# A two-layer graph transformer on one core: in layer 2, P normalised before its transposes, and PV with V stationary in 64x32 tiles

## The reference

```python
q = (x @ Wq.T).reshape(b, n, 12, 32); k = (x @ Wk.T)...; v = (x @ Wv.T + bv)...
scores = einsum('bqhd,bkhd->bhqk', q, k) * scale + (adj + adj)[:, None]
row_nonzero = any(scores != 0, axis=-1, keepdims=True)
p = nan_to_num(softmax(where(row_nonzero, scores, -inf), axis=-1))
out = einsum('bhqk,bkhd->bqhd', p, v).reshape(b, n, 384) @ Wo.T + bo
x = layernorm(x + out)
```

## Time and profile before

| | |
|---|---|
| median of three runs | 1967.26 us (1966.64 to 1967.50) |
| profiled execution | 1970.78 us, of which 1968.9 us are the span of the profile |
| TensorE busy | 96% of the span |
| DVE, ACT, POOL busy | 64%, 54%, 20% |
| HBM read and written | 102 GB/s over the span |

### The profile page before, as it was taken

How to read it: one execution, slowest core, us unless ns; L and a number is a source line. 1 busy time by engine, 2 the same in 40 slices (tenths; PEclk the granted TensorE clock), 3 DMA queues, 4 the chain that set the end, 5 groups by cost and what they waited for, 6 DMA issues and landing times.

```text
span 1968.9 us, 55169 instructions
## 1 busy us (share of the span) xinstructions
PE 1899.2 (96%) x20816; PEld 1867.3 (95%) x20816; DVE 1261.6 (64%) x2478; ACT 1056.1 (54%) x2270; POOL 402.3 (20%) x552
## 2 busy tenths in 40 slices
PE   6699999999999999999999999988799999999997
PEld 6699999999999999999999999988799999999997
DVE  5565666666666666666666666655566667666675
ACT  4364555655556545565455654554355555555555
POOL 0111112121221212212122111211121222222222
PEclk9799999999999999999999999999899999999999
DMA  7533444444444344444444444333322232222322
GB/s 184 151 110 108 116 129 110 123 114 122 123 111 129 107 127 118 113 127 109 128 117 115 124 111 127 109 104 97 94 77 76 83 88 83 78 78 84 88 80 67
DMA packets 268505, 213.60 MB, mean 108 GB/s; under 512 B 142640, under 2 KB 250928, under 8 KB 268464
## 3 DMA queue, kind: packets, MB, share of 16 engines
q1 hardware_dynamic: 268464, 213.05, 39.5%
HBM read 120.33 MB, written 79.69 MB: 102 GB/s over the span
## 4 chain that ended last, share of the span: by engine, by line
PE 90%; DMA 3%; DVE 3%; SPq 3%; ACT 1%; issue 1%; POOL 0%; ACTq 0%; POOLq 0%; DVEq 0%
PE a_bank L441 29%; PE a_banks L441 28%; PE b_bank L1423 16%; PE b_banks L1423 5%; PE b_bank L1490 2%; PE a_bank L490 2%; PE b_banks L1477 2%; PE b_banks L1467 2%; PE a_banks L510 2%; SPq L262 1%; PE b_bank L1500 1%; DMA a_work<-x_turned 1%; DMA ctx_turned<-a_work 0%; DMA xt_raw<-in_xT 0%; DMA x_turned<-a_work 0%
## 5 line engine op out<-in xcount | busy, mean ns | idle before, releaser
L441 PE MATMUL a_bank<-a_x1t_hi,a_w_hi 128*128 128x256 f32 x1152 | 327.9, 285 | 20.3 <-DVE a_x1t_lo L912 20.3
L441 PE MATMUL a_bank<-a_x1t_hi,a_w_lo 128*128 128x256 f32 x1152 | 324.7, 282 | 0.0
L441 PE MATMUL a_bank<-a_x1t_lo,a_w_hi 128*128 128x256 f32 x1152 | 324.4, 282 | 0.0
L729 ACT ACTIVATE a_work<-a_bank,a_b 128x256 f32<-128x256 f32 x384 | 160.3, 468 | 203.4 <-PE a_bank L441 203.0
L441 PE MATMUL a_banks<-a_w_hi,a_hid_hi 128*128 128x384 f32 x768 | 258.8, 337 | 0.4 <-DVE a_hid_lo L927 0.4
L441 PE MATMUL a_banks<-a_w_hi,a_hid_lo 128*128 128x384 f32 x768 | 258.2, 336 | 0.0
L441 PE MATMUL a_banks<-a_w_lo,a_hid_hi 128*128 128x384 f32 x768 | 258.2, 336 | 0.0
L927 DVE TENSOR_TENSOR a_hid_lo<-a_work,a_hid_hi 128x512 fp32r<-128x512 f32 x192 | 131.6, 698 | 190.4 <-ACT a_hid_hi L734 190.4
L441 PEld LDWEIGHTS a_bank<-a_x1t_hi,a_w_hi 128*128 128x128 f32 x1152 | 220.7, 192 | 23.2 <-DVE a_x1t_lo L912 21.3
L441 PEld LDWEIGHTS a_bank<-a_x1t_lo,a_w_hi 128*128 128x128 f32 x1152 | 221.3, 192 | 0.0
L441 PEld LDWEIGHTS a_bank<-a_x1t_hi,a_w_lo 128*128 128x128 f32 x1152 | 220.0, 191 | 0.0
(11 more groups left out here) (176 smaller groups left out, 5494.6 us busy)
## 6 DMA issues: line engine op xcount, KB each, us to landing
a_work<-in_x SPq DMA_DIRECT2D x64, 384.0 KB, 3.3
p_turned<-a_work SPq DMA_DIRECT2D x256, 64.0 KB, 2.3
a_work<-p_turned SPq DMA_DIRECT2D x32, 512.0 KB, 3.3
xt_raw<-in_xT SPq DMA_DIRECT2D x32, 384.0 KB, 4.0
ctx_turned<-a_work SPq DMA_DIRECT2D x256, 48.0 KB, 1.7
a_work<-ctx_turned SPq DMA_DIRECT2D x32, 384.0 KB, 3.5
x_turned<-a_work SPq DMA_DIRECT2D x256, 48.0 KB, 1.7
a_work<-x_turned SPq DMA_DIRECT2D x32, 384.0 KB, 3.9
```

The source lines that it names most:

```text
L441: r = pe.matmul(out, lhs[a], rhs[b], start=first and n == 0, stop=last and n == 2)
L729: r = act.activation(silu[:, p % 2, s * GROUP:(s + 1) * GROUP], A[p % 3][:, s * GROUP:(s + 1) * GROUP], ACT.Silu, bias=b1[:, m:m + 1])
```

## The change

The sum of a row of P is taken by DVE after the exponential (`invert_sum`: a reduction, the reciprocal, the mask), and POOL multiplies P with it (`scale_p`) before P is turned. The column of ones and the zeros between heads go, and with them the two memsets; V keeps its natural rows (`v_rows`). `pv` has V of one head as the stationary operand (64 rows by 32 columns) and 64 moving columns of P turned, 48 matmuls in 64x32 tiles; its result is the context already turned, so `take_ctx` and `turn_ctx` go. `ctxt_high` and `ctxt_low` split it in four pieces of 256 columns, in two calls r. `turn_p` moves from the end of step g to step g + 1, between the two tiles of `values`; `take_k` goes, and ACT copies K with Q (`take_q` for u = 0, 1, 2). `Wo` of layer 2 is loaded head by head in another order, by 12 transfers.

```diff
             def load_next():
                 sp.wait_ge(o_mm, TILES * NG)
-                for i, piece in enumerate(next_pieces):
-                    load_piece(sp, piece, next_loaded[i], by_block=i < 3)
+                for i, piece in enumerate(next_pieces[0:3]):
+                    load_piece(sp, piece, next_loaded[i], by_block=True)
+                for n in range(H1):
+                    r, hp = divmod(n, H1 // 2)
+                    k, j = divmod(n, P // DH1)
+                    sp.dma_start(stage(next_pieces[3])[j * DH1:(j + 1) * DH1, k, :],
+                                 next_w["Wo"][(2 * hp + r) * DH1:(2 * hp + r + 1) * DH1, :]).then_inc(next_loaded[3], 16)
...
-        QK_BANK = (1, 0, 2)
-        V_BANK, PV_BANK, TURN_BANK = (3, 1), (2, 0), (3, 2)
+        QK_BANK = (0, 1, 2)
+        V_BANK, PV_BANK = (0, 1), (2, 3)
+        CTX_ROWS = (((0, P, 0), (0, P // 2, 1)), ((P // 2, P, 1), (0, P, 2)))
...
             def qk(g, u):
                 if u == 0:
                     pe.wait_ge(xt_lo, g + 1)
+                    wait(pe, v_done, TILES * (g - 1) + 1)
+                elif u == 1:
                     wait(pe, v_done, TILES * g)
-                elif u == 1:
-                    wait(pe, ctx_done, TILES * (g - 1))
                 else:
-                    wait(pe, ctxt_lo, TILES * (g - 1))
+                    wait(pe, ctxt_lo, 2 * (g - 2) + 1)
...
             def turn_p(g, t):
-                if t == 0:
-                    pe.wait_ge(biased, TILES * (g + 1))
-                pe.wait_ge(exp_done, TILES * g + t + 1)
+                pe.wait_ge(p_scaled, TILES * g + t + 1)
                 wait(pe, y_done, TILES * (g - 1) + t + 1)
...
+            def wait_for_pv(g):
+                pe.wait_ge(pt_done, TILES * (g + 1))
+                for t in range(TILES):
+                    pe.wait_ge(v_swapped[t], 32 * (g + 1))
+                pe.wait_ge(v_kept, TILES * (g + 1))
+                wait(pe, ctxt_lo, 2 * g)
+
+            def pv(g, t):
+                for s in range(2):
+                    n = TILES * t + s
+                    for h in range(H1 // 2):
+                        for r in range(2):
+                            k, i = divmod(r * (H1 // 2) + h, ROWS)
+                            at = (k - r) * GROUP + n * NODES
+                            rows = slice(64 * r, 64 * r + 64)
+                            m = pe.matmul(one[PV_BANK[r]][32 * i:32 * i + 32, at:at + NODES], v_rows[rows, n, h * DH1:(h + 1) * DH1],
+                                          pt[rows, t, h * P + 64 * s:h * P + 64 * s + 64], start=True, stop=True,
+                                          skip_group_check=True)
+                m.then_inc(pv_mm, 1)
...
             # TensorE's step
-                if front:
-                    for t in range(TILES): values(g, t)
-                if back:
-                    for t in range(TILES): pv(b, t, front)
+                if front: values(g, 0)
+                if back:
+                    for t in range(TILES): turn_p(b, t)
+                if front: values(g, 1)
+                if back: wait_for_pv(b)
                 if front: scores(g, back)
-                if front and more: qk(g + 1, 0)
-                if back:
-                    for t in range(TILES): turn_ctx(b, t, front)
-                if front and more: qk(g + 1, 1)
+                if back:
+                    for t in range(TILES): pv(b, t)
+                if front and more:
+                    for u in range(3): qk(g + 1, u)
                 if back:
                     for t in range(TILES): attn_out(b, t, front)
-                if front and more: qk(g + 1, 2)
-                if front:
-                    for t in range(TILES): turn_p(g, t)
...
             # ACT's step, the calls in their new order
+                square(g - 2, 0..1), take_pt(b, 0..1), xt_high(g + 1), ctxt_high(b, 0..1), keep_v(g, 0..1), norm(g - 2),
+                take_q(g + 1, 0), exp(g, 0), take_q(g + 1, 1), exp(g, 1), take_q(g + 1, 2)
...
             # DVE
+            def invert_sum(g, t):
+                s = prob[:, t, :].rearrange("p (h n) -> p h n", h=H1)
+                dve.wait_ge(exp_done, TILES * g + t + 1)
+                dve.tensor_reduce(psum[:, t, :], s, AX_X, ALU.add).then_inc(summed, 1)
+                dve.wait_ge(summed, TILES * g + t + 1)
+                wait(dve, p_scaled, TILES * (g - 1) + t + 1)
+                dve.reciprocal(rden[:, t, :], psum[:, t, :]).then_inc(rden_done, 1)
+                dve.wait_ge(rden_done, TILES * g + t + 1)
+                dve.wait_ge(magnitude, TILES * g + t + 1)
+                dve.scalar_tensor_tensor(out=rden[:, t, :], in0=samax[:, t, :], scalar=0.0, in1=rden[:, t, :],
                                          op0=ALU.is_gt, op1=ALU.mult).then_inc(rden_masked, 1)
...
             # DVE's step, the calls in their new order
+                take_v(g, 0..1), xt_low(g + 1), ctxt_low(b, 0), add_adj(g, 0..1), find_max(g, 0..1), ctxt_low(b, 1),
+                find_magnitude(g, 0), invert_sum(g, 0), find_magnitude(g, 1), invert_sum(g, 1), finish(b)
...
             # POOL, after both calls of shift
+            def scale_p(g, t):
+                s = prob[:, t, :].rearrange("p (h n) -> p h n", h=H1)
+                pool.wait_ge(rden_masked, TILES * g + t + 1)
+                pool.tensor_tensor(s, s, rden[:, t, :].unsqueeze(2).broadcast_to([P, H1, NODES]), ALU.mult).then_inc(p_scaled, 1)
```

More of the change, by code:

```diff
@@ L1443, in values @@
             def values(g, t):
-                if t == 0:
-                    wait(pe, ctxt_lo, TILES * (g - 1))
-                else:
-                    pe.wait_ge(q_done, 2 * g + 1)
+                pe.wait_ge(q_done, 3 * g + t + 1)
                 for k in range(KT):
@@ L1509, in attn_out @@
+            def attn_out(g, t, front):
+                if t == 0:
+                    pe.wait_ge(ctxt_lo, 2 * (g + 1))
+                    if front:
+                        pe.wait_ge(biased, TILES * (g + 2))
+                for k in range(KT):
+                    r = mm3(two[t][:, 0:D], [ctx_t[j][:, k, t * P:(t + 1) * P] for j in range(2)],
                             [W["Wo"][j][:, k, :] for j in range(2)], k == 0, k == KT - 1)
@@ L1536, in step @@
                         attn_out(b, t, front)
-                if front and more:
-                    qk(g + 1, 2)
-                if front:
-                    for t in range(TILES):
-                        turn_p(g, t)
             step(0, back=False)
@@ L1599, in _ @@
             last["scalar"][0]()
-            for u in range(2):
+            for u in range(3):
                 take_q(0, u)
             last["scalar"][1]()
-            act.wait_ge(pairs_zeroed, 1)
-            act.wait_ge(ones_set, 1)
             def step(g, front=True, back=True, late=True, more=True):
                 b = g - 1
+                if late:
+                    for t in range(TILES):
+                        square(g - 2, t)
+                if back:
+                    for t in range(TILES):
+                        take_pt(b, t)
                 if front and more:
                     xt_high(g + 1)
+                if back:
+                    for r in range(2):
+                        ctxt_high(b, r)
                 if front:
@@ L1613, in step @@
                 if late:
-                    for t in range(TILES):
-                        square(g - 2, t)
+                    norm(g - 2)
                 if front and more:
                     take_q(g + 1, 0)
-                if back:
-                    for t in range(TILES):
-                        ctxt_high(b, t)
-                if late:
-                    norm(g - 2)
                 if front:
-                    for t in range(TILES):
-                        exp(g, t)
+                    exp(g, 0)
                 if front and more:
@@ L1628, in step @@
                 if front:
-                    for t in range(TILES):
-                        take_pt(g, t)
+                    exp(g, 1)
+                if front and more:
+                    take_q(g + 1, 2)
             step(0, back=False, late=False)
@@ L1732, in step @@
                 if back:
-                    for t in range(TILES):
-                        take_ctx(b, t)
+                    ctxt_low(b, 0)
                 if front:
@@ L1785, in step @@
                         shift(g, t)
+                    for t in range(TILES):
+                        scale_p(g, t)
             step(0, back=False, late=False)
```

122 lines of the change are left out of this document (44 added, 78 removed).

## The result

In the same runs the kernel after took 1973.0 us (median of 7, 1967.97 to 1974.3) and the one before 1965.93 us (median of 7, 1964.55 to 1967.5). The ratio is 1.0032, with an interval of 1.0021 to 1.0044: the change made the kernel **slower, by 0.3%**. Forecast was 1965.4 us, 0.1% faster. The measured time lies inside the range and on the other side of the sign.

A forecast was written before the change was run, and what follows sets the result against it. TensorE's queue bounds the old kernel (17.65 us a group), DVE's order the new (17.36). Loop -8.8, drain +7.0, fill -0.1 make -1.9 us: 1968.9 from the profiled 1970.78, 1965.4 on the median's scale; range 1946 to 1982.

The forecast's parts named there:

- Branch b: Each step, DVE's finish and means, ACT's square, then take_pt: next scores at 16.17 us, giving a period of 17.36.
- Branch a: Each step, POOL's second product, turn_p of tile 1, second half of V: next scores could start at 16.06 us.
- rival 2: PV slow from uneven tiles: over 1.30 us, each tenth costs 3 us; at 1.8, +14, 1981 us; chance 0.25.
- its means are done 1.4 later: DVE in each step: the means end 1.4 us after finish starts at 11.97, so at 13.4.
- 30 such periods: Layer 2's loop, scores of group 1 to group 31: 30 equal periods, changing from 17.65 to 17.36 us, -8.8 in all.
- attn_out 3.1: End of layer 2: the last attn_out takes 3.1 us, from 19.7 to 22.8 after the last scores.
- +7.0: End of layer 2: last y 23.2 us after the last scores in place of 16.22, 7.0 us more.
- Rival 3: Granted clock drops in a few loop groups because TensorE now idles 0.6 us a group: 2000 us; chance 0.05.
- -1.9: Whole kernel: loop -8.8, drain +7.0 and fill -0.1 us, summed against the profiled 1970.78 us.

The follow-up runs named there:

- square_later: Against the kernel after, ACT's squares moved behind take_pt and xt_high: 1942.43 us, ratio 0.9893 to the kernel before.
- adj_first: Against the kernel after, DVE adds adj to the scores ahead of ctxt_low(b, 0): 1942.1 us, ratio 0.9885 to the kernel before.
- the repeat: Later profiled executions of the same two kernels, nothing changed: the kernel after 1972.76 us, ratio 1.0026; one execution of the kernel before 1964.35 us.

## Why the prediction was wrong

Each step, counted from the end of the scores as in the prediction, in the step shown above:

| step | forecast | measured |
|---|---|---|
| PV, first load to the next stage | 1.30 | 1.14 |
| add_adj starts | 2.92 | 2.60 |
| finish starts | 11.97 | 11.44 |
| POOL's second product ends | 13.59 | 12.97 |
| means done | 13.4 | 13.06 |
| take_pt starts | 14.6 | 14.32 |
| take_pt ends | 16.11 | 15.80 |
| next scores load | 16.17 | 16.23 |
| period | 17.36 | 17.42 |

**The mechanism held.** Branch b sets the period: ACT's square waits for DVE's means and `take_pt` follows it, as the prediction said, and `square_later` proved it by removing it. TensorE's own work was forecast at 16.75 us, and `adj_first`, where nothing waits, runs at 16.55. Branch a, forecast to be ready 0.11 us before branch b, came 0.6 us sooner than that and costs TensorE only the 0.14 us at `turn_p`.

**PV (rival 2) was fine.** 16 loads on the busiest tile at 58 ns were 0.93 us in the prediction (1.35 us over 24 loads is 56 ns, which makes it 0.90), and the 96 loads spread over 0.95 (1.05 with the last one's length). That the busiest tile sets this is not shown: the scores, with 12 loads on each of eight tiles, would take 0.7 us by the same rule and take 0.99, so the close number may be luck. The Trainium skill's overhead of 60 cycles for each matmul (TensorEngine Tiling (Array Packing), Instruction Overhead), an estimate of 0.6 us more a group, doesn't show: PV has twice the matmuls, now on eight tiles, and is 0.41 us shorter.

The first numbers that failed are those of the loop, whose gain was forecast at 8.8 us and measured 4.9 (4.7 in the repeat).

**The period** was 0.09 us too short in 27 steps, 2.4 us in all. Two terms hid each other. The steps up to `finish` ran 0.5 us ahead of the forecast, 0.3 of them up to `add_adj`, since PV and ACT's first pieces were quicker, and 0.2 in reciprocal and mask, 0.4 to 0.5 us each time in place of 0.55. Against that, "its means are done 1.4 later" took 1.62, as POOL's product, which is new, holds DVE's first mean by 0.30; and from the end of `take_pt` to the first load of the scores I took 0.06 where it is 0.43.

**"30 such periods"** took no account of passes that differ: scores 2 to scores 3 cost 1.7 us more than 17.36, by a stop at new code. With the 2.4 this is the 4 us that the loop lacks.

**The end** was the larger failure in kind. "attn_out 3.1" was a price at full clock. Its loads took 4.77 and 5.29 us, at a granted clock of 0.59 and 0.50, after waits of TensorE that the new order itself makes longer. The forecast +7.0 became +9.2 (+10.9 between the repeats), the residual 25.4 us after the last scores in place of 23.2. Of these 2.2 us attn_out(31) makes 1.8; it starts 0.4 us later than forecast. In the repeat it starts another 0.6 us later, since attn_out(30) was wholly at the lower clock, and the residual, the means, the squares and `take_pt` follow it. The trace that the forecast rests on had this price in it, in its own attn_out(30) at 0.64. Rival 3 named the clock, and looked for it in the loop, where 0.7 us of idle time a step left it at 1.00.

**The sum.** -1.9, plus 3.9 to 4.1 in the loop, plus 2.2 to 3.9 at the end, is +4.2 to +6.1 against +7.1 by the medians; the last 1 to 3 us stay open. A gain and a loss of 7 to 9 us, with errors of 2 to 4 us in each, can't fix the sign. No single rival came true.

What the forecast did not see is what the change could have been. It named the squares as the last link of the chain, but its own sum would have given their swap only 0.11 us a step, because branch a stood at 16.06. The swap gave 0.80, as branch a was forecast 0.6 us too late. It could be read from the trace of the kernel after, and not from the forecast.

## What to carry to other kernels

When a change lengthens a chain through engines that are mostly idle, look at what each of them has queued ahead of the link and at what each waits for first: here one swap of order on ACT, or one on DVE, was worth over 25 us of 1970, some four times what the change cost. Price the last steps by themselves, with TensorE's work after a wait taken at the lower granted clock as well as at the full one. And count the loop's passes apart from its first.

## What the runs showed of the hardware

- A DVE `tensor_scalar` on 128x2 values lasts until POOL's `tensor_tensor` on 128x768 ends: 474 ns where it takes 169 alone. In the same step DVE's `b_y` (one input in PSUM, 0.56 us) beside that product was not held.
- Short matmuls whose code runs for the first time stop: 1.60 and 1.70 us within one PV of 96 loads, 0.42 in the loop's first pass, none after. Each stop ends 2.3 to 2.7 us after a 16 KB packet of the instruction queue starts.
- 96 loads of 64x32 tiles, on eight tiles unevenly, spread over 0.95 us, and 96 of 32x64 tiles, evenly, over 0.99. What sets either is open.
- Two attn_outs of the last steps took up to 5.3 us after waits and 2.89 with TensorE kept busy: at a granted clock of 0.50 to 0.66, and at 1.00.
